# Half-precision pairs for the value chunks of a depthwise convolution

## The reference

```python
xn = layernorm over channels of groupnorm(x)
q  = dwconv3x3(conv1x1(xn, q_w),  q_dw)      # 96 channels
kv = dwconv3x3(conv1x1(xn, kv_w), kv_dw)     # 48 channels: 24 of k, 24 of v
k, v = split(kv)
q, k = l2norm(q), l2norm(k)                  # over the 16384 pixels
attn = softmax(q @ k.T * temperature)        # 8 heads of 12 channels, 2 key/value groups
x = x + conv1x1(attn @ v, proj_w)
x = x + conv1x1(concat(conv1x1, conv3x3, conv5x5, dilated conv3x3)(groupnorm(x)), wf)
```

## Time and profile before

| what | value |
|---|---|
| median of 3 runs | 1664.78 us (1664.5 to 1666.73) |
| the profiled execution | 1664.77 us |
| its span, first to last instruction | 1663.0 us |
| PE busy | 1605.5 us, 97% |
| DVE busy | 1456.9 us, 88% |
| ACT busy | 1040.2 us, 63% |
| POOL busy | 655.7 us, 39% |
| granted TensorE clock, mean | 0.975 of full |

### The profile page before, as it was taken

How to read it: one execution, slowest core, us unless ns; L and a number is a source line. 1 busy time by engine, 2 the same in 40 slices (tenths; PEclk the granted TensorE clock), 3 DMA queues, 4 the chain that set the end, 5 groups by cost and what they waited for, 6 DMA issues and landing times.

```text
span 1663.0 us, 38439 instructions
## 1 busy us (share of the span) xinstructions
PE 1605.5 (97%) x13933; PEld 1524.3 (92%) x13933; DVE 1456.9 (88%) x1949; ACT 1040.2 (63%) x1667; POOL 655.7 (39%) x507
## 2 busy tenths in 40 slices
PE   6999989999999999999999999899999999899998
PEld 5999959999999986999999996899999999599998
DVE  6788789999789959999978986999988897799996
ACT  4877676555286868645546776765446677765651
POOL 4888031222289303232248903023226950312232
PEclk9999979999999997999999998899999999799999
DMA  7012205666502202666630220366661131054553
GB/s 197 0 42 73 71 5 138 171 164 180 151 18 59 81 16 48 158 169 178 171 101 15 73 67 1 89 175 176 170 167 48 34 85 36 16 137 127 145 149 100
DMA packets 105042, 166.37 MB, mean 100 GB/s; under 512 B 40266, under 2 KB 78763, under 8 KB 104780
## 3 DMA queue, kind: packets, MB, share of 16 engines
q1 hardware_dynamic: 81772, 138.95, 33.1%
q10 hardware_dynamic: 23168, 26.04, 5.1%
HBM read 52.20 MB, written 25.17 MB: 47 GB/s over the span
## 4 chain that ended last, share of the span: by engine, by line
PE 80%; DVE 9%; issue 6%; ACT 3%; SPq 1%; DMA 1%; DVEq 0%; ACTq 0%
PE ps L1017 41%; PE ps L869 14%; PE ps L844 12%; PE ps L874 7%; PE ps L902 3%; DVE region L1765 1%; PE ps L1012 1%; DVE region L1493 1%; ACT region L1237 1%; DVE region L1340 1%; ACT region L1168 1%; DVE region L1790 1%; ACT region L1193 1%; DVE region L1762 1%; ACT region L1218 0%
## 5 line engine op out<-in xcount | busy, mean ns | idle before, releaser
L1017 PE MATMUL ps<-region,W 128*96 128x256 f16 (+2 forms) x7140 | 790.6, 271 | 16.0 <-DVE region L1790 8.0
L1017 PEld LDWEIGHTS ps<-region,W 128*96 128x96 f16 (+1 forms) x7140 | 779.1, 122 | 19.8 <-DVE region L1790 9.5
L1493 DVE TENSOR_TENSOR region<-V,ps 128x2322 int32<-128x2322 int32 (+2 forms) x104 | 246.9, 2384 | 37.0 <-issue 30.9
L1237 ACT ACTIVATE region<-region 96x1584 f16<-96x1584 f32 (+2 forms) x80 | 98.4, 1272 | 287.5 <-DVE region L1699 287.5
L748 POOL TENSOR_TENSOR region<-region 96x528 f32<-96x528 f32 (+1 forms) x72 | 96.4, 1343 | 437.9 <-DVE region L1765 238.5
L869 PE MATMUL ps<-region 128*128 (+2 forms) x2160 | 248.7, 276 | 8.6 <-DVE region L1493 4.7
L869 PEld LDWEIGHTS ps<-region 128*128 128x128 f32 x2160 | 243.7, 192 | 12.4 <-issue 7.5
L844 PE MATMUL ps<-proj,region 96*128 96x240 f32 x1024 | 208.5, 367 | 0.0
L844 PEld LDWEIGHTS ps<-proj,region 96*128 96x128 f32 x1024 | 194.6, 190 | 12.8
L667 POOL TENSOR_TENSOR region<-region,cbias 128x576 f32 (+1 forms) x124 | 175.7, 1417 | 57.9 <-DVE region L1465 54.2
L738 POOL TENSOR_TENSOR region<-region,X 96x1536 f32<-96x1536 f32 x40 | 116.0, 2901 | 190.1 <-DVE region L1820 190.1
(11 more groups left out here) (249 smaller groups left out, 2139.8 us busy)
## 6 DMA issues: line engine op xcount, KB each, us to landing
region<-region SPq DMA_DIRECT2D x104, 247.5 KB, 4.2
region<-in_x_dram SPq DMA_DIRECT2D x128, 192.0 KB, 2.4
out_dram<-region SPq DMA_DIRECT2D x40, 576.0 KB, 4.3
region<-region ACTq DMA_DIRECT2D x72, 247.5 KB, 2.5
X<-in_x_dram SPq DMA_DIRECT2D x30, 576.0 KB, 6.2
region<-region SPq DMA_DIRECT2D x32, 247.4 KB, 5.1
X<-in_x_dram SPq DMA_DIRECT2D x19, 384.0 KB, 10.4
region<-region SPq DMA_DIRECT2D x24, 185.6 KB, 3.9
```

Source lines behind the costliest of these rows:

```text
L1017: last = mm(o, w, src, start=opens and k == 0, stop=k == len(steps) - 1, skip_group_check=g in (2, 4) or split and ck > 0)
L1237: act.activation(dst[0:C, a:e, x:z], src, ACT.Copy, scale=1.0 if whole else col(SA)).then_inc(s_h, 1)
L1493: v.tensor_tensor(T[:, i, 3 * c:3 * c + m].bitcast(i32).rearrange("p m (i j) -> p m i j", j=3), taps.broadcast_to([P, m, BW // 3, 3]), mas ...
```

## The change

`SPLIT` gets the four value chunks, 20 to 23, and `SPLIT_RUNS` a third run. So from the second image on POOL splits sixteen chunks, and PE multiplies the value chunks by 16-bit pairs. Value taps get a scale of their own, `VKS`: two DVE reductions find the largest sum of value taps (counted in `N_QKS`), and five small DVE steps make `VKS` and its inverse `VUN` after the other scales. ACT's copy of the value taps uses `VKS`, and ACT's copy of a value chunk out of PSUM multiplies by `VUN`, in all four images. Three columns of `small` are used a second time for it.

```diff
-        SPLIT = (2, 4, 5, 7, 8, 10, 11, 13, 14, 16, 17, 19)
-        SPLIT_RUNS = (slice(2, 18, 3), slice(4, 20, 3))
+        SPLIT = (2, 4, 5, 7, 8, 10, 11, 13, 14, 16, 17, 19, 20, 21, 22, 23)
+        SPLIT_RUNS = (slice(2, 18, 3), slice(4, 20, 3), slice(20, 24))
...
+        VTMAX, VKS, VUN = BMAX, WMAX, QSC
...
-        N_BOUND, N_RES, N_QKS, N_AMAX, N_WSC = 6, 9, 23, 28, 31
-        N_QKV = N_WSC + len(OSCS) + 3
+        N_BOUND, N_RES, N_QKS, N_AMAX, N_WSC = 6, 9, 25, 30, 33
+        N_QKV = N_WSC + len(OSCS) + 8
...
-                    act.activation(V[:, :, 3 * QK:], V[:, :, 3 * QK:], ACT.Copy, scale=col(QINV, P)).then_inc(s_vscaled, 1)
+                    act.activation(V[:, :, 3 * QK:], V[:, :, 3 * QK:], ACT.Copy, scale=col(VKS, P)).then_inc(s_vscaled, 1)
...
-                                       ps[:, bank:bank + 2, 0:3 * H], ACT.Copy).then_inc(s_qd, 1)
+                                       ps[:, bank:bank + 2, 0:3 * H], ACT.Copy, scale=col(VUN, P)).then_inc(s_qd, 1)
...
+            link(setup, v.tensor_reduce(tapsum[:, 0:KC], rawdw[:, 3 * QK:3 * CO, :].rearrange("p (c m) d -> p c (m d)", m=3), AX.X,
+                                        ALU.add, apply_absolute_value=True))
+            link(setup, v.tensor_reduce(col(VTMAX, P), tapsum[:, 0:KC], AX.X, ALU.max))
             assert setup.n == N_QKS
             statistics(6, len(TAKEN))
...
             link(setup, v.tensor_tensor(col(QKS, P), col(QKS, P), col(QINV, P), ALU.mult))
+            link(setup, v.tensor_scalar(col(VTMAX, P), col(VTMAX, P), 1e-20, None, ALU.max))
+            link(setup, v.tensor_scalar(col(VTMAX, P).bitcast(i32), col(VTMAX, P).bitcast(i32), 0x7F800000, None, ALU.bitwise_and))
+            link(setup, v.reciprocal(col(VKS, P), col(VTMAX, P)))
+            link(setup, v.tensor_scalar(col(VKS, P), col(VKS, P), 2.0 ** 7, None, ALU.mult))
+            link(setup, v.tensor_scalar(col(VUN, P), col(VTMAX, P), col(QINV, P), 2.0 ** -7, ALU.mult, ALU.mult))
```

## The result

The changed kernel takes **1652.93 us** (median of 4 runs, 1652.22 to 1654.32) where the kernel before takes 1664.64 (4 runs, 1663.03 to 1666.73): 11.7 us less, a ratio of 0.993 with a 95% interval of 0.9913 to 0.9947. The prediction was 1655.5, with a range from 1653.8 to 1660.0. The interval stands for 8.8 to 14.5 us less and still holds the sum's 9.3; the first round of experiments gives 9.7 to 14.0 and doesn't.

The account below looks back on a forecast made before the run. The prediction took PE to bound the kernel, with DVE close behind in the depthwise stage. Pairs -9.9 us and setup +0.6 gave -9.3 against 1664.77, so 1655.5 us, range 1653.8 to 1660.0.

Parts of the forecast that it names:

- PE, the main term: Value chunks, images two to four: 3.14 us a chunk by pairs against 4.03, saving 3.57 us an image without other waits.
- the last part of the prediction: Signs to look for: 12.8 us from chunk 20's start to the group mean, some 0.2 us wait at chunk 22.
- rivals 2 and 4: Value chunks: 2, pairs at loop's pace, 1659.9, chance 0.06; 4, weight loads set pace, 1685.4, chance 0.05.
- Rival 3: Depthwise stage: the clock takes the gain, one value chunk an image at 1.2 GHz; 1664.9 us, chance 0.04.
- DVE's gate on the value chunks: Depthwise stage: bands make chunk 22 start 0.25 us late, leaving 3.3 us saved an image, 9.9 in three.
- Next in line, POOL: After chunk 23, mean and grams shift along without loss; POOL's four more splits end 15 us before chunk 20, costing nothing.
- The 5 us kept for POOL: Range allowance in case POOL's longer work slows the depthwise chunks beside it; the forecast itself took zero.
- ACT: Scaled eviction of value chunks: zero cost on the path; 0.8 us an image, should the scale double it, still covered.
- Setup: Two reductions in DVE's chain, 0.38 and 0.2 us, together +0.6 (0.3 to 0.85); five later steps covered.
- The packing: First image: a third run of 1.2 to 1.7 us fits DVE's 1.85 us wait for ACT; uncovered at most 0.1.
- Sum: Whole kernel: -9.9 + 0.6 = -9.3 us against 1664.77, giving 1655.5 us.
- How the numbers follow: Chances and range: low 1653.8 from no DVE gate, setup 0.3, some clock tenths; high 1660.0 from POOL and rival pace.

Follow-up runs that it names:

- the first round of experiments: Both kernels run again without edit: the changed kernel 1653.97 us, ratio 0.9929 (0.9916 to 0.9942) to the kernel before.
- the experiment on the first image: Changed kernel with the first image's value chunks in pairs too, reductions moved, twelve spare matmuls: 1655.02 us, ratio 0.994; with packing moved earlier and five spare matmuls 1650.46.
- the second pair of traces: Profiles of both kernels run again without edit: kernel before 1664.83 us, ratio 0.9996; changed kernel 1653.97 us, ratio 0.9929.
- scales_only: Changed kernel with its reductions, scales and scaled evictions, but value chunks in 32 bits: 1663.73 us, ratio 0.9993 to the kernel before.

## Why the prediction was right in kind and wrong in size

**Pace of the pairs (step "PE, the main term"): right.** 3.14 us a chunk where no wait is in it, 58 ns a matmul, in all three images. From chunk 20 (581.66 + 3.14 = 584.80) to the mean it is 12.83 us, where the last part of the prediction wanted 12.8. With it fall rivals 2 and 4, and the Trainium skill's 81 ns ("TensorE: Matmul & The Clock Gate", section "Back-to-back issue gap"), by which the kernel would have become slower. The trace had 58 before and has 58 after. Rival 3 falls with the granted clock of 1.00 in the stage.

**DVE's gate on the value chunks: right.** 0.27 us of waiting in the chain where 0.25 was worked out, the bands within 0.04 us of the times given. One reading on the way was wrong, without harm: the 0.17 us at 544.11 is PE's idle time, not the step from DVE's end to PE's start. DVE ended at 544.01 there, so the step is the 0.1 that was taken; at chunk 22 it is 0.15 (591.18 to 591.33). The depthwise stages became shorter by 3.28, 3.45 and 3.33 us, 10.06 in all, against 9.9.

**Next in line, POOL: right.** The mean and the grams follow at once, 0.14 us apart. POOL's last split ends near 569.7, 60 us after the first began:

```profile
568.61 1.06 POOL L695 COPY region<-region 128x768 f16<-128x768 f16 x1
621.28 2.97 POOL L715 TENSOR_TENSOR region<-X 96x512 f32<-96x512 f32 x2 [51.61 <-PE ps L938]
```

The 5 us kept for POOL were not needed. In the experiment on the first image POOL was the bound, though: there it had to start late.

**ACT: right on the path, and the scale has a price.** The scaled eviction takes 0.90 us instead of 0.81:

```profile
597.83 0.90 ACT L1130 ACTIVATE region<-ps,small 128x768 f32<-128x768 f32 x1 [2.24 <-PE ps L875]
```

It is hidden, as reckoned. The Trainium skill, page "ScalarE: Activation LUTs", section "What ACT_TABLE_LOAD costs", says that a per-partition operand adds about 93 ns to an `ACTIVATE`; the two rows agree, with 0.09 us.

**Setup: right.** The two reductions take what was assumed, 0.38 and 0.18 us. The first projection starts 0.84 us later in this pair of traces, the end of the range (0.85), where 0.6 was taken; over the nine traces with the old setup or the new it is 0.67 in the mean:

```profile
30.42 0.38 DVE L1378 TENSOR_REDUCE region<-region 128x24 f32<-128x216 f32 x1
30.83 0.18 DVE L1380 TENSOR_REDUCE small<-region 128x1 f32<-128x24 f32 x1
...
41.21 0.48 PE L819 MATMUL ps<-small,gmean 96*96 96x1 f32 x2 [2.97 <-DVE small L1419]
```

**The packing: hidden.** The third run takes 1.4 us (213.19 to 214.62), and DVE still waits 0.39 for ACT behind it, where it waited 1.85:

```profile
214.20 0.42 DVE L1521 COPY V<-region 128x72 f16<-128x72 f16 x3
215.02 0.28 DVE L1580 SCALAR_TENSOR_TENSOR region<-region,ps 120x120 f32<-120x120 f32 x1 [0.39 <-ACT region L1178]
```

**The step that failed** is the "Sum", with the low end in "How the numbers follow". The sum held the convolution stages, half of the span, to be the same before and after, because no instruction of theirs was changed. They gave 2.90 us in the two profiled executions. Of these, 1.63 are the late slow stretch of the fourth image and 1.20 are waits of PE later in the first and fourth image; in the second pair of traces two late slow stretches make 3.27 of 3.37. The runs fit this: the kernel before gains 2.4 us by spare matmuls that bring the changed kernel next to nothing. The sum with the measured terms is -10.06 + 0.84 - 0.37 - 2.90 = -12.49, the difference of the two spans. Without the last term it is -9.6, and the pair of kernels with five spare matmuls stands 10.0 apart. For the low end, the prediction had allowed "some tenths from the clock". It had looked for the clock in the depthwise stage and the attention output, and not at the trace's own rows of the convolution stages, where the same work took 202.2 us in two images and 203.5 and 204.3 in the others. Those four numbers stood in the trace of before. They show what these stages could give without any cause in the change (3.4 us, if all four came to 202.2), and the low end should have gone there, to about 1652. That the change would remove these losses, and not move them to other images, couldn't be read from that trace; for the prediction, the larger gain is luck.

**What stays open.** What sets the time from the last 1.2 GHz stretch of the attention output to the convolution stage, which sorts slow heads and late slow stretches. Also, how much of the 2.4 us that the five spare matmuls bring in the kernel before is theirs, and how much that of the code loads which they shift. And the 0.37 us in the grams of the second image: they take 19.96 or 19.97 us there in all five traces with the old scales and 19.59 or 19.60 in the nine with the new ones, scales_only among them, so the pairs don't make it. It is one wait for DVE, before and after:

```profile
617.81 0.34 PE L923 MATMUL ps<-region 24*96 24x24 f32 x2 [0.76 <-DVE region L1579]
```

```profile
614.22 0.34 PE L924 MATMUL ps<-region 24*96 24x24 f32 x2 [0.39 <-DVE region L1588]
```

## What to carry to other kernels

Where the trace already has the new form of an instruction beside the old one, the price of a substitution can be read closely from it: here 9.9 us were forecast for three stages and 10.06 measured. The larger error lay in places that the change doesn't touch. So compare repeated stages of the same kernel with each other before fixing a range: images that do the same work in 202.2 and in 204.3 us show how much the total can move without any cause in the change. And when an engine is given less to do, follow the helpers too: the first image gained only after the packing ahead of POOL's splits had been moved forward by ten rounds of DVE's loop.

## What the runs showed of the hardware

- A wait may cost more than its length: behind a wait of 1.82 to 2.46 us, in a stage with a fast head, PE was granted 1.2 GHz for 3.4 us in 7 of 11 cases, at about 1.6 us each. The length of the wait alone doesn't decide it: four waits of 2.40 to 2.45 us had no such stretch behind them, nor had one of 1.81 in a stage with a late 25th matmul. In stages with slow heads, where the wait was 1.1 to 1.8 us, nothing was lost behind it (0 of 21).
- Whether the granted clock fell at the head of a stage went with the time since it had last been low: 22 of 22 stages that began 5.7 to 7.2 us after a 1.2 GHz stretch were granted 1.2 GHz again at their head, and none of the 34 that began 2.4 to 5.64 us after it.
- Program code comes by DMA, 16 KB at a time, and can delay the kernel's own small transfers: in the second image, 33 KB took 2.5 to 3.1 us beside such a load and 1.9 to 2.0 without. The Trainium skill, page "Runtime: NRT & Kernel Launch", section "Instruction fetch mechanics", gives blocks of 16 KiB, 256 instructions, and calls the cost of crossing one mostly hidden. The blocks agree with the packets. The cost was not hidden here: the 25th matmul of the stage came 0.6 to 1.3 us late in 16 of the 26 stages with a load at their head.
- So adding instructions in one place can change the time in another. 144 more on PE moved the code loads from the heads of the first and third image to those of the second and fourth.
- Spare matmuls that fit into the wait (1.28 us in one of at least 1.4) took 2.4 us off the kernel before. More than twice as many (2.84 us) pushed back the work behind the wait and made the changed kernel 1.4 to 2.5 us slower than with few or none.
- DVE's packing of 72 elements, nine instructions, took 1.5 us late in the stage, while POOL stood idle, and 2.5 us earlier in it, while POOL was busy with the weights.
